# GpSimd gathers the second tile's rows ahead of its wait for the stored gates

## The reference, cut to what matters

```python
x = x + _L0_conv_ref(_ln_c(x), w3, w7, w15, w_mix)
t = _to_tokens(x)                       # 2048 tokens of 512 features
# the experts, on the normalised tokens, 8 experts, 2 of them for each token
router_logits = x @ gate_w.T
routing_probs = softmax(router_logits)
topk_w, topk_idx = top_k(routing_probs, 2); topk_w /= sum(topk_w)
h = silu(x @ w1[e]) * (x @ w3[e])       # 512 -> 1024
y = h @ w2[e]                           # 1024 -> 512
out = sum over the two experts of y * weight
t = t + out
```

## Time and profile before

| | |
|---|---|
| median of three runs | 848.08 us (847.98 to 848.32) |
| span of the profiled execution, first to last instruction | 845.4 us |
| PE busy in the span | 791.5 us (94%) |
| DVE, ACT, POOL busy in the span | 351.7, 318.6, 268.8 us |
| mean granted TensorE clock | 0.970 |

### The profile page before, as it was taken

How to read it: one execution, slowest core, us unless ns; L and a number is a source line. 1 busy time by engine, 2 the same in 40 slices (tenths; PEclk the granted TensorE clock), 3 DMA queues, 4 the chain that set the end, 5 groups by cost and what they waited for, 6 DMA issues and landing times.

```text
span 845.4 us, 13004 instructions
## 1 busy us (share of the span) xinstructions
PE 791.5 (94%) x3764; PEld 655.6 (78%) x3765; DVE 351.7 (42%) x791; ACT 318.6 (38%) x487; POOL 268.8 (32%) x313
## 2 busy tenths in 40 slices
PE   4999999628999999999999999999999999999993
PEld 3777888527888888888888888888888888888882
DVE  5886758685113621172216223511361172244111
ACT  6784755432214512262127125311441262262120
POOL 4346210003233422361216315322341262243311
PEclk9999999659999999999999999999999999999997
DMA  7247678628111811173116513712281164111111
GB/s 237 47 75 138 150 162 175 256 105 326 25 31 34 317 39 25 27 263 95 32 30 201 159 25 88 271 25 37 46 302 37 25 224 136 25 37 25 30 32 25
DMA packets 55873, 91.72 MB, mean 108 GB/s; under 512 B 7344, under 2 KB 40496, under 8 KB 49712
## 3 DMA queue, kind: packets, MB, share of 16 engines
q1 hardware_dynamic: 45728, 71.64, 27.2%
q0 software_dynamic: 9408, 19.42, 12.0%
q10 hardware_dynamic: 720, 0.46, 0.2%
HBM read 64.97 MB, written 18.15 MB: 98 GB/s over the span
## 4 chain that ended last, share of the span: by engine, by line
PE 86%; DVE 7%; DMA 2%; issue 2%; ACT 1%; POOL 0%; POOLq 0%; ACTq 0%; DVEq 0%
PE bank L720 23%; PE bank L718 23%; PE bank L719 23%; PE bank L734 4%; PE bank L631 3%; PE bank L632 3%; PE bank L633 3%; PE bank L712 2%; PE bank L653 1%; DMA xg<-xn_rows,gather_at 1%; DVE bn L782 1%; DVE wc_lo L823 1%; PE bank L671 1%; PE bank L646 1%; DVE mv L791 1%
## 5 line engine op out<-in xcount | busy, mean ns | idle before, releaser
L718 PE MATMUL bank<-w_hi,xT_hi 128*128 128x512 f32 x576 | 229.0, 398 | 4.3 <-DVE xT_lo L1019 4.3
L720 PE MATMUL bank<-w_hi,xT_lo 128*128 128x512 f32 x576 | 225.9, 392 | 0.0
L719 PE MATMUL bank<-w_lo,xT_hi 128*128 128x512 f32 x576 | 225.2, 391 | 0.0
L1042 DVE TENSOR_TENSOR h<-bank,h 128x512 f32<-128x512 f32 x72 | 49.8, 692 | 294.0 <-PE bank L720 293.8
L718 PEld LDWEIGHTS bank<-w_hi,xT_hi 128*128 128x128 f32 x576 | 108.9, 189 | 26.3 <-DVE xT_lo L1019 4.7
L720 PEld LDWEIGHTS bank<-w_hi,xT_lo 128*128 128x128 f32 x576 | 108.7, 189 | 23.4
L719 PEld LDWEIGHTS bank<-w_lo,xT_hi 128*128 128x128 f32 x576 | 108.9, 189 | 21.8
L718 PE MATMUL bank<-w_hi,hT_hi 128*128 128x512 f32 x288 | 118.7, 412 | 0.0
L559 ACT ACTIVATE h<-bank 128x512 f32<-128x512 f32 x72 | 43.1, 599 | 197.4 <-PE bank L720 197.4
L720 PE MATMUL bank<-w_hi,hT_lo 128*128 128x512 f32 x288 | 112.6, 391 | 0.0
L719 PE MATMUL bank<-w_lo,hT_hi 128*128 128x512 f32 x288 | 112.3, 390 | 0.0
(11 more groups left out here) (145 smaller groups left out, 924.2 us busy)
## 6 DMA issues: line engine op xcount, KB each, us to landing
w_raw<-in_units SPq DMA_DIRECT2D x48, 1024.0 KB, 5.9
joint<-xs_parts SPq DMA_DIRECT2D x64, 128.0 KB, 3.8
out_x<-XT SPq DMA_DIRECT2D x17, 256.0 KB, 3.6
XT<-in_x SPq DMA_DIRECT2D x16, 256.0 KB, 7.0
xn_rows<-xnb SPq DMA_DIRECT2D x16, 256.0 KB, 2.5
xg<-xn_rows,gather_at POOLq DMA_INDIRECT x37, 3.4
out_x<-y,add_at POOLq DMA_INDIRECT x36
gate_row<-gate_rows,gate_at POOLq DMA_INDIRECT x36
```

Source lines behind the costliest of these rows:

```text
L718: pe.matmul(B[bank][:], stat_hi, hi, start=start, stop=False)
L719: pe.matmul(B[bank][:], stat_hi, lo, start=False, stop=False)
L720: return pe.matmul(B[bank][:], stat_lo, hi, start=False, stop=stop)
L1042: dve.tensor_tensor(h[:, j, :], B[2 * j + 1][:], h[:, j, :], ALU.mult).then_inc(h_out, 1)
```

## The change

GpSimd's copy of the second tile's indices, the waits that belong to it and the gather of the second tile's rows are moved ahead of the wait for the stored gates and of the gather of the first tile's gates. No instruction is added or removed.

```diff
             gather(src_i[:, 0:1])
             pool.wait_ge(tables_ready, 1)
+            pool.tensor_copy(gather_at[:], src_i[:, bass.ds(column(1), 1)]).then_inc(gather_index, 1)
+            pool.wait_ge(xg_ps, 1)
+            pool.wait_ge(gather_index, 1)
+            gather(gather_at[:, 0:1])
             pool.wait_ge(gate_st, 16)
             gather_gates(gate_i[:, 0:1])
-            pool.wait_ge(xg_ps, 1)
-            pool.tensor_copy(gather_at[:], src_i[:, bass.ds(column(1), 1)]).then_inc(gather_index, 1)
-            pool.wait_ge(gather_index, 1)
-            gather(gather_at[:, 0:1])
             pool_tile(0, 1, 2, 1)
```

## The result

The changed kernel takes 844.05 us in the median of four runs (843.81 to 844.34), the kernel before 848.03 in four beside it (847.32 to 848.32). The ratio is 0.9955 with a 95% interval of 0.9944 to 0.9967: faster by 4.0 us, 0.45%. The direction and the place were right, the size was too small by 1.6 us.

A forecast was written before the change was run, and what follows sets the result against it. PE was taken to bound the kernel, busy 791.5 of 845.4 us. The wait gave -2.40 and copy, gates, DVE and `h` were taken as 0: 848.08 - 2.40 = 845.7 us, range 845.2 to 847.0.

The forecast's parts named there:

- The wait, 2.40 us: PE's wait for the second tile's gathered rows at the transposes (L712) goes whole: -2.40 us.
- Copy and gather: On GpSimd, the moved index copy ends at 188.1, the gather follows at 188.4 and lands at 191.8; cost 0.
- DVE unmoved: DVE's work beside the moved copy and gather isn't delayed: `xT_lo` stays at 187.93, cost 0.
- gates: The first tile's gates' gather stays near 193.8; their landing, 0 to 0.63 us later, costs PE nothing.
- the second half of `h`: DVE makes it for `turn_h(1)` 0.18 us before PE needs it; loss 0 to 0.1 us, taken as none.
- A: PE's wait for the second tile's rows goes only in part; 846.9 us if half stays; chance 0.04.
- B: VectorE waits for GpSimd's moved copy and issue, delaying `xT_lo`: 847.0 us (chance 0.04) or 849.8 us (0.03).
- C: The time stays at 848.1 us: releases come later than read, or unprofiled runs lack PE's wait; chance 0.03.
- The granted clock is 1.00 through the wait, so there is no clock to be won or lost there: At PE's wait for the second tile's rows, the clock adds no gain or loss: 0 us.
- The median of the runs lies 2.7 us above that span and I keep this distance: For the whole kernel, the 2.7 us between profiled span and median stays, so span 843.0 gives 845.7 us.
- The low end of the forecast: Bottom of the whole kernel's forecast range, 845.2 us, from 0.4 us of run-to-run difference in weights and gather sharing engines.

The follow-up runs named there:

- a4: Kernel before, with the second tile's copy and gather put ahead of the gates' gather but still behind the wait for the stored gates; 847.26 us, ratio 0.9997.
- c3: The kernel before, unchanged, profiled once more; the profiled execution took 847.90 us.
- b3: Kernel before, with the second tile's copy and gather held besides until the first tile's gates have landed; 852.25 us, ratio 1.0053.
- c2: Kernel before, with the second tile's copy and gather held until DVE has made the first expert's last low half; 850.97 us, ratio 1.0037.
- b2: Changed kernel, with GpSimd's copy and gather held until DVE has made the first tile's `xT_lo`; 844.21 us, ratio 0.9961 to before.
- b4: Changed kernel, with DVE making the first tile's `xT_lo` and the first `h` ahead of low halves of weights; 843.26 us, ratio 0.9953 to before.
- b1: Kernel before, with SP holding the second expert's weight loads until PE has turned the second tile's rows; 844.09 us, ratio 0.9961.
- a3: Kernel before, with only the copy of the second tile's indices moved ahead of the wait for the gates; 845.02 us, ratio 0.9971.

## Why the prediction was right or wrong

- **The wait, 2.40 us: right.** The distance from the first to the last transposes fell from 642.5 to 640.0, by 2.5, in executions with the clock at 1.00.
- **Copy and gather: right, within 0.7 us.** Forecast were a copy from 186.0 to 188.1 and a landing at 191.8 in the time of the first profile, 0.66 us less in that of the profile after: 185.3, 187.4 and 191.1. The copy ran from 185.6 to 187.4, to the end of its `w_lo`, and the rows landed at 191.8, 10 us ahead of PE. The gather followed its copy by 0.77 us; the 0.27 of the forecast was read in the old place.
- **DVE unmoved, gates and the second half of `h` without cost: right.** `xT_lo` kept its 2.94 us behind `gate_i`; POOL's gather of the gates started at 193.64, 0.5 us later than before in the same time; no wait took the place of the old one. Rivals A, B and C didn't happen.
- **"The granted clock is 1.00 through the wait, so there is no clock to be won or lost there": wrong, and this is the step that failed.** It was read from one execution. In two of five profiles of before the clock fell to half behind this wait and took 1.6 us more, and 38 of 98 runs have the mean clock that goes with it. 38/98 of 1.6 is 0.6 us; with 2.5 for the wait that makes 3.1, against 3.4 between the medians of all runs (847.50 and 844.08). The last 0.3 us have no cause named here.
- **"The median of the runs lies 2.7 us above that span and I keep this distance": wrong, the same mistake seen from the sum.** 1.7 us of it lie around the span in every run. The other 1.0 was the difference between an execution without the fall and runs that had it, and with the wait it went too. For the three runs of the forecast this is argued from their times, since no clock is on record for them: they took 847.98 to 848.32, and of the 20 runs of before at 847.97 or more that have one, 19 are at 0.968. That three such runs came together, and with them 848.03 as the median beside the result, is chance; it is why 4.0 us were measured (2.5 and 1.6 make 4.1) where all runs give 3.4. Within the profiles the sum closes: taking 2.5 from the profiled execution's own 847.1 gives 844.6; with its late lead-in of 0.66 us it gives 843.9, against 844.15 in the profile.

The low end of the forecast was 0.4 us under 845.7, which is 845.3 and not 845.2; neither reaches 844.05, as the range had no term for the clock.

What remains open: why the clock falls behind one standstill of 2.4 us and not behind the next one of the same length.

## What to carry to other kernels

Price a standstill of TensorE by more than its length: take several profiles of the unchanged kernel and look at the granted clock behind it, since a part of the executions may pay for it twice. Compare the mean granted clock of the profiled execution with that of the other runs too: here two thousandths told the executions with the fall from those without it. When the median of the runs lies well above the time of the profiled execution, or the runs are spread to one side only, the profile shows a lucky execution, and the difference may belong to something that the change removes. Here the gather that needs only its indices belonged ahead of the wait for other data and ahead of the bulk loads of another queue; moved past its neighbour alone (a4) it gave nothing, as its index copy then ran beside VectorE.

## What the runs showed of the hardware

- The granted clock can fall some time after TensorE has started again: in c3 work began at 203.91 at full clock, which fell near 205.1. Behind standstills of 5.4 and 4.6 us work began at half clock (b3 and c2); in c2 the stretch from 204 to 206 has a mean of 0.72 while PE stood until 206.12, so it had fallen before the work began; behind those of 2.2 to 2.4 us the clock fell in two of five profiles of before, 1.2 us late.
- A copy of one column on GpSimd takes 0.18 us, and 1.42, 1.79, 2.27 or 2.33 us (before, changed, a4, b2) where a `w_lo` of VectorE with two SBUF inputs was under way; each time it ended 0.03 to 0.05 us behind that operation. In b4, where VectorE was idle just then, the same copy took 0.18. The `w_lo` beside them took 2.28 to 2.29 us throughout. The Trainium skill, "SBUF — State Buffer", section "SBUF: two separate sides", describes the lock; the trace agrees for the side on which VectorE starts first.
- The gather's landing counted from the end of its issue took 5.5 to 6.1 us among the weight loads and 2.5 without them (b1). Before it was 8.33 - 2.74 = 5.59, and in a3 7.98 - 1.86 = 6.12.
